# The q, k and v products of a windowed attention layer, from f32 matmuls to three f32r terms

## What is computed

```
h   = emb[x] + 2 * (lora_A[:, x].T @ lora_B.T)
n   = layernorm(h)
q, k, v = split(n @ Wqkv + bqkv)            # 16 heads of 16
local   = softmax over keys within 64 tokens of the query, times v
global  = softmax over the first 64 keys, times v of the first 64 tokens
h   = h + ((1 - g) * local + g * global) @ Wout + bout,  g = sigmoid(n @ Wg + bg)
h   = h + ffn(layernorm(h))                  # 8 experts, 2 per token, capacity 1.25
```

## Time and profile before

| | |
|---|---|
| Median of 3 runs | 3883.29 us (3879.36 to 3885.97) |
| The profiled execution: its own time | 3882.32 us |
| Its span, first to last instruction | 3880.6 us |
| PE busy | 3481.5 us (90% of the span), 47537 matmuls |
| PEld busy | 2753.0 us (71%), 47537 loads |
| DVE, ACT, POOL busy | 2172.5 (56%), 1868.3 (48%), 2324.1 us (60%) |
| Mean granted clock of PE | 0.952 |

### The profile page before, as it was taken

How to read it: one execution, slowest core, us unless ns; L and a number is a source line. 1 busy time by engine, 2 the same in 40 slices (tenths; PEclk the granted TensorE clock), 3 DMA queues, 4 the chain that set the end, 5 groups by cost and what they waited for, 6 DMA issues and landing times. The chain is left out here.

```text
span 3880.6 us, 117579 instructions
## 1 busy us (share of the span) xinstructions
PE 3481.5 (90%) x47537; PEld 2753.0 (71%) x47537; DVE 2172.5 (56%) x5392; ACT 1868.3 (48%) x3086; POOL 2324.1 (60%) x2599
## 2 busy tenths in 40 slices
PE   2898889888888888888899849999999999999998
PEld 1555555555555555555555539999999999999998
DVE  3576767767676776767677634343434344443333
ACT  0455555555555555555555624343444444444343
POOL 5566777777777777777776645444544444444443
PEclk7899999999999999999999969999999999999999
DMA  4354544445454444545454323232323233222222
GB/s 142 123 157 117 163 122 151 130 138 139 128 152 123 150 133 135 144 125 149 124 154 130 109 87 65 50 68 46 71 48 72 48 69 72 46 51 45 45 45 41
DMA packets 242540, 398.31 MB, mean 103 GB/s; under 512 B 34572, under 2 KB 150748, under 8 KB 242044
## 3 DMA queue, kind: packets, MB, share of 16 engines
q1 hardware_dynamic: 168540, 297.43, 25.0%
q0 software_dynamic: 70512, 91.16, 13.8%
q10 hardware_dynamic: 3008, 2.95, 0.2%
HBM read 198.55 MB, written 192.88 MB: 101 GB/s over the span
## 5 line engine op out<-in xcount | busy, mean ns | idle before, releaser
L1388 POOL DMA_INDIRECT out_y<-out_t,tok_out x264 | 425.7, 1612 | 747.3 <-DMA out_y<-out_t,tok_out 405.0
L1534 ACT ACTIVATE act<-psS 128x512 f32<-128x512 f32 x528 | 316.9, 600 | 882.1 <-PE psS L1462 880.9
L1596 DVE TENSOR_TENSOR h_lo<-act,h_hi 128x512 fp32r<-128x512 f32 x528 | 367.2, 695 | 562.3 <-ACT h_hi L1535 543.8
L993 DVE TENSOR_REDUCE negm<-psS 128x4 f32<-128x640 f32 x512 | 418.8, 818 | 452.3 <-remote 276.3
L903 ACT ACTIVATE pl<-psS 128x896 f32<-128x896 f32 x512 | 467.7, 913 | 379.9 <-PE psS L741 372.0
L568 POOL TENSOR_SCALAR_AFFINE_SELECT pl<-pl 128x512 f32<-128x512 f32 x512 | 354.3, 692 | 448.4 <-ACT pl L903 446.2
L1497 PE MATMUL psO<-w_hi,h_hi 128*128 128x256 f32 x2112 | 598.8, 284 | 0.8 <-DVE h_lo L1596 0.8
L1497 PE MATMUL psO<-w_lo,h_hi 128*128 128x256 f32 x2112 | 588.7, 279 | 0.0
L1497 PE MATMUL psO<-w_hi,h_lo 128*128 128x256 f32 x2112 | 587.6, 278 | 0.0
L1462 PE MATMUL psS<-xg_hi,w_hi 128*128 128x256 f32 x1984 | 551.7, 278 | 0.0
L1462 PE MATMUL psS<-xg_hi,w_lo 128*128 128x256 f32 x1984 | 551.5, 278 | 0.0
(11 more groups left out here) (232 smaller groups left out, 7728.6 us busy)
## 6 DMA issues: line engine op xcount, KB each, us to landing
qk_scr<-qk SPq DMA_DIRECT2D x64, 768.0 KB
Q<-qk_scr SPq DMA_DIRECT2D x128, 384.0 KB
K<-qk_scr SPq DMA_DIRECT2D x128, 384.0 KB
qk_scr<-qk SPq DMA_DIRECT2D x64, 512.0 KB
qk_scr<-qk SPq DMA_DIRECT2D x64, 256.0 KB
h_rows<-held SPq DMA_DIRECT2D x32, 512.0 KB
hb<-h_rows SPq DMA_DIRECT2D x32, 512.0 KB
x_rows<-x SPq DMA_DIRECT2D x32, 512.0 KB
```

Source lines behind the costliest of these rows:

```text
L993: dve.tensor_reduce(negm[:, g, 0, v, :, 2 * half:2 * half + 2], psS[:, 2:4, 0:2 * BAND].rearrange("p a (q u) -> p a q u", u=BAND), AX.X, A ...
L1388: pool.indirect_dma_start(out=y[:, :], in_=out_t[:, tile.out, s, :], in_offset=None, out_offset=bass.IndirectOffsetOnAxis(ap=tok_out[:, ti ...
L1534: act.activation(act32[:, b, :, 0:cols], src, ACT.Silu)
L1596: dve.tensor_tensor(h_lo[:, 2 * b:2 * b + 2, 0:cols], act32[:, b, :, 0:cols], h_hi[:, 2 * b:2 * b + 2, 0:cols].bitcast(F32), ALU.subtract) ...
```

## The change

- The weights of q and k (`wqk`) and of v (`wv_sb`) become two F32R tiles each, `*_hi` (the rounded value) and `*_lo` (what is left), made in the setup by DVE.
- The transposed rows `xn_t` become `xn_hi` and `xn_lo`, both F32R. ACT writes `xn_hi` from the PSUM bank and DVE, in a new stage `xn_lo`, subtracts it from the bank into `xn_lo`. PE's later stages wait for `xn_lo_done`, and the bank is free only then.
- Each product becomes three matmuls: hi by hi, and the two of hi by lo.
- Both row tiles have 64 more columns in front that repeat the first 64 tokens. So `values` 2 takes 128 columns of rows (the first 64 tokens twice) as weights against all 256 columns of `wv`, in 6 matmuls where there were 4 products (8 instructions), and ACT picks its half of the columns.
- All five lists in `ORDER` are laid out anew, and their starting points move, which is why some flags differ. POOL's is shown whole; of PE's and DVE's the stretch around `xn_t` and `qk`.

```diff
-        wv_sb = keep("wv_sb", [P, KT, D])
+        wv_hi = keep("wv_hi", [P, KT, D], F32R)
+        wv_lo = keep("wv_lo", [P, KT, D], F32R)
...
-        wqk = keep("wqk", [P, KT, 4, P])
+        wqk_hi = keep("wqk_hi", [P, KT, 4, P], F32R)
+        wqk_lo = keep("wqk_lo", [P, KT, 4, P], F32R)
...
+                    dve.tensor_copy(wv_hi[:, :, :], wv_raw[:, :, :])
                     for k in range(KT):
                         for s in range(2):
-                            dve.tensor_copy(wqk[:, k, 2 * s:2 * s + 2, :].rearrange("p a (d h) -> p a d h", d=HD),
-                                            wqk_raw[:, k, s * D:(s + 1) * D].rearrange("p (h a d) -> p a d h", a=2, d=HD))
+                            ins = dve.tensor_copy(wqk_hi[:, k, 2 * s:2 * s + 2, :].rearrange("p a (d h) -> p a d h", d=HD),
+                                                  wqk_raw[:, k, s * D:(s + 1) * D].rearrange("p (h a d) -> p a d h", a=2, d=HD))
+                    ins.then_inc(w_cut, 1)
+                    dve.wait_ge(w_cut, 1)
+                    dve.tensor_tensor(wv_lo[:, :, :], wv_raw[:, :, :], wv_hi[:, :, :].bitcast(F32), ALU.subtract)
+                    for k in range(KT):
+                        for s in range(2):
+                            dve.tensor_tensor(wqk_lo[:, k, 2 * s:2 * s + 2, :].rearrange("p a (d h) -> p a d h", d=HD),
+                                              wqk_raw[:, k, s * D:(s + 1) * D].rearrange("p (h a d) -> p a d h", a=2, d=HD),
+                                              wqk_hi[:, k, 2 * s:2 * s + 2, :].rearrange("p a (d h) -> p a d h", d=HD).bitcast(F32),
+                                              ALU.subtract)
...
-            xn_t = tmp("xn_t", [P, KT, T])
+            xn_hi = tmp("xn_hi", [P, KT, SIDE + T], F32R)
+            xn_lo = tmp("xn_lo", [P, KT, SIDE + T], F32R)
...
-                            wv = wv_sb[:, :, :].rearrange("p k (v a d) -> p k a v d", a=2, d=HD)
-                            pe.wait_ge(xn_t_done, KT * (s + 1))
+                            pe.wait_ge(xn_lo_done, KT * (s + 1))
                             take(key, v_done, 3 * s + arg + 1)
                             if arg < 2:
                                 for j in range(2):
-                                    tok = slice((2 * arg + j) * P, (2 * arg + j + 1) * P)
+                                    tok = slice(SIDE + (2 * arg + j) * P, SIDE + (2 * arg + j + 1) * P)
                                     for k in range(KT):
-                                        last = pe.matmul(psX[:, b, j * D:(j + 1) * D], xn_t[:, k, tok], wv_sb[:, k, :],
-                                                         start=(k == 0), stop=(k == KT - 1))
+                                        for n, (x_, w) in enumerate(((xn_hi, wv_hi), (xn_hi, wv_lo), (xn_lo, wv_hi))):
+                                            last = pe.matmul(psX[:, b, j * D:(j + 1) * D], x_[:, k, tok], w[:, k, :],
+                                                             start=(k == 0 and n == 0), stop=(k == KT - 1 and n == 2))
                             else:
                                 for k in range(KT):
-                                    for a in range(2):
-                                        last = pe.matmul(psX[64 * a:64 * (a + 1), b, 0:P], xn_t[:, k, 0:64], wv[:, k, a, :, :],
-                                                         start=(k == 0), stop=(k == KT - 1))
+                                    for n, (x_, w) in enumerate(((xn_hi, wv_hi), (xn_hi, wv_lo), (xn_lo, wv_hi))):
+                                        last = pe.matmul(psX[:, b, 0:D], x_[:, k, 0:2 * SIDE], w[:, k, :],
+                                                         start=(k == 0 and n == 0), stop=(k == KT - 1 and n == 2))
                             last.then_inc(v_ready, 1)
...
-                            take(key, xn_t_done, KT * s + arg + 1)
+                            take(key, xn_lo_done, KT * s + arg + 1)
...
-                            pe.wait_ge(xn_t_done, KT * (s + 1))
+                            pe.wait_ge(xn_lo_done, KT * (s + 1))
                             take(key, qk_rest_done, 4 * s + arg + 1)
                             for k in range(KT):
-                                last = pe.matmul(psX[:, b, :], wqk[:, k, arg, :], xn_t[:, k, :],
-                                                 start=(k == 0), stop=(k == KT - 1))
+                                for n, (w, x_) in enumerate(((wqk_hi, xn_hi), (wqk_hi, xn_lo), (wqk_lo, xn_hi))):
+                                    last = pe.matmul(psX[:, b, :], w[:, k, arg, :], x_[:, k, SIDE:SIDE + T],
+                                                     start=(k == 0 and n == 0), stop=(k == KT - 1 and n == 2))
                             last.then_inc(qk_ready, 1)
...
-                                                         psX[rows, b, 0:P].rearrange("p (v d) -> p v d", d=HD), ACT.Copy)
+                                                         psX[rows, b, 0:D].rearrange("p (v a d) -> p v a d", a=2, d=HD)[:, :, a, :], ACT.Copy)
...
-                            act.activation(xn_t[:, arg, :], psX[:, b, :], ACT.Copy).then_inc(xn_t_done, 1)
+                            act.activation(xn_hi[:, arg, 0:SIDE], psX[:, b, 0:SIDE], ACT.Copy)
+                            act.activation(xn_hi[:, arg, SIDE:SIDE + T], psX[:, b, :], ACT.Copy).then_inc(xn_hi_done, 1)
...
+                        if stage == "xn_lo":
+                            dve.wait_ge(xn_hi_done, KT * s + arg + 1)
+                            if arg == 0:
+                                need(dve, v_ready, 3 * s)
+                                need(dve, qk_ready, 4 * s)
+                            x_ = psX[:, BANK["xn_t", arg, s], :]
+                            dve.tensor_tensor(xn_lo[:, arg, 0:SIDE], x_[:, 0:SIDE], xn_hi[:, arg, 0:SIDE].bitcast(F32), ALU.subtract)
+                            dve.tensor_tensor(xn_lo[:, arg, SIDE:SIDE + T], x_, xn_hi[:, arg, SIDE:SIDE + T].bitcast(F32),
+                                              ALU.subtract).then_inc(xn_lo_done, 1)
...
 ORDER["pe"]
-                ("nxt", "max", 11), ("far", "xn_t", 0), ("far", "xn_t", 1), ("nxt", "exp", 0), ("nxt", "max", 12), ("far", "qk", 0),
-                ("nxt", "exp", 1), ("far", "qk", 1), ("far", "qk", 2), ("nxt", "max", 13), ("far", "qk", 3), ("nxt", "exp", 2),
...
+                ("nxt", "m_rows", 1), ("cur", "out", 11), ("nxt", "values", 2), ("far", "xn_t", 0), ("nxt", "max", 11),
+                ("far", "xn_t", 1), ("nxt", "exp", 0), ("nxt", "max", 12), ("nxt", "exp", 1), ("far", "qk", 0), ("far", "qk", 1),
+                ("nxt", "max", 13), ("far", "qk", 2), ("far", "qk", 3), ("nxt", "exp", 2), ("nxt", "max", 14), ("cur", "mix", 0),
...
 ORDER["dve"]
-                ("nxt", "kg", 2), ("prev", "top", 0), ("nxt", "max", 11), ("nxt", "max", 12), ("far", "qk", 0), ("far", "zgate", 0),
-                ("far", "qk", 1), ("prev", "top", 1), ("far", "qk", 2), ("nxt", "max", 13), ("far", "qk", 3), ("nxt", "max", 14),
...
+                ("nxt", "max", 11), ("far", "xn_lo", 0), ("far", "xn_lo", 1), ("past", "rank", 5), ("prev", "top", 2),
+                ("nxt", "max", 12), ("nxt", "kg", 0), ("far", "qk", 0), ("far", "qk", 1), ("nxt", "max", 13), ("prev", "top", 3),
+                ("far", "qk", 2), ("far", "qk", 3), ("nxt", "max", 14), ("cur", "mix", (0, 0)), ("nxt", "cut", (2, 0)),
...
             ORDER["pool"] = (
-                ("nxt", "hold", 0), ("far", "gather", 5), ("cur", "sel", 0), ("cur", "sel", 1), ("nxt", "hold", 1),
-                ("nxt", "qk3", 0), ("nxt", "qk3", 1), ("nxt", "qk3", 2), ("nxt", "qk3", 3), ("cur", "sel", 2), ("prev", "mix", 0),
-                ("cur", "sel", 3), ("old", "scatter", 4), ("old", "scatter", 5), ("prev", "mix", 1), ("cur", "sel", 5),
-                ("cur", "sel", 6), ("prev", "mix", 2), ("prev", "mix", 3), ("far", "gather", 6), ("cur", "sel", 7),
-                ("nxt", "hold", 2), ("cur", "sel", 8), ("far", "gather", 7), ("old", "scatter", 6), ("nxt", "hold", 3),
-                ("cur", "sel", 10), ("old", "scatter", 7), ("cur", "sel", 11), ("cur", "sel", 12), ("prev", "rstd2", None),
-                ("cur", "sel", 13), ("past", "scatter", 0), ("past", "scatter", 1), ("cur", "sel", 15), ("cur", "sel", 16),
-                ("cur", "sel", 17), ("next", "gather", 0), ("far", "rstd1", None), ("cur", "sel", 18), ("next", "gather", 1),
-                ("past", "scatter", 2), ("next", "gather", 2), ("next", "gather", 3), ("past", "scatter", 3), ("next", "gather", 4),
+                ("prev", "sel", 12), ("prev", "sel", 13), ("past", "rstd2", None), ("far", "gather", 0), ("prev", "sel", 15),
+                ("prev", "sel", 16), ("prev", "sel", 17), ("nxt", "rstd1", None), ("prev", "sel", 18), ("far", "gather", 1),
+                ("far", "gather", 2), ("far", "gather", 3), ("far", "gather", 4), ("old", "scatter", 0), ("nxt", "hold", 0),
```

(6 more changed lines are left out.)

98 lines of the change are left out of this document (50 added, 48 removed).

## The result

The changed kernel takes 3894.9 us, median of 12 runs (3880.3 to 3914.5). The kernel before takes 3879.1 in its 12 (3873.8 to 3888.3). The ratio is **1.0042**, 95% interval 1.0024 to 1.0059: a little slower, where the forecast was 3835 and faster. The profiled execution has a span of 3897.1 us, 16.5 more than before. Its marker line runs from 274.4 to 2289.1 (before, 268.2 to 2272.3): 6.2 us come ahead of the first marker and 10.6 between the first and the last, 0.34 a sequence. The expert part, with the same code, has the rest, -0.3.

What follows compares the result with a forecast made beforehand. PE was taken to bound the attention part (886.0 of 1000 us busy). Terms of -1.6 us a sequence, 32 times, gave -51 us; with +3 for setup and +1, 3882.3 became 3835 us, range 3775 to 3905.

Steps and rivals of the forecast that it cites:

- The products as such: PE's q and k products: 24 f32r matmuls at 0.27 us a step, 6.5 us a sequence in place of 8.4.
- The lists: 0: New order of all lists priced at 0 us a sequence (-1.0 to +1.5); POOL's run of seven stays, three pairs become four scatters.
- the clock falls a second time in a period: Sign that the forecast is wrong: the four scatters in a row bring a second low clock in each period.
- my first rival: Late hop: ACT's and DVE's signals each 1.9 us late, +1.6 us a sequence, 3937 us; chance 0.18 with milder forms and scatters.
- PE time taken out is on the path: At the qk stages other engines wait for PE, so PE time saved there shortens the period.
- My terms for the arithmetic: For one sequence: q and k -1.9, values -0.7 and +0.3, hop +0.6, DVE's extra work +0.1; sum -1.6 us.
- The values' -0.4: PE's value products: values 0 and 1 -0.7 us a sequence, values 2 +0.3.
- q and k's -1.9: q and k products gain 1.9 us a sequence (1.5 to 2.3), with 20% of steps slow before and after.
- The hop: +0.6: New ACT-to-DVE-to-PE step xn_lo ahead of qk costs 0.6 us a sequence (+0.2 to +1.3).
- The rival of "hidden": POOL's burst and the maxima around it end the period, PE waits longer for negm; no change, 3886 us, chance 0.10.
- Setup: Five subtractions and a copy on DVE in the setup add 3 us once.
- the third rival: Weight loads not hidden: each product term adds its 188 ns load, +8.8 us a sequence, 4168 us; chance 0.02.

Runs made afterwards that it cites:

- f32_new_lists: Kernel before (old arithmetic) with the changed kernel's lists, without the xn_lo steps; 3671.4 us on a quiet chip, 3949.3 us on a stalling one.
- changed_again_2: The changed kernel as it is, run again on a quiet chip; 3643.5 us against 3677.8 for the kernel before.
- terms_old_lists_2: The changed arithmetic with the old lists, xn_lo put behind max 11, on a stalling chip; 3889.7 us against 3893.0 for the kernel before, 0.9993.

## Why the prediction was wrong

*The products as such: the step was nearly right, the size hangs on the clock.* 0.242 us a step on average (median 0.232), where I had 0.27, and 0.228 at the high clock. The mean is even above my upper bound of 0.238, since the first step of a stage takes 0.34 (1332.86 to 1333.20). Line 812's steps have the priced 0.12. In the result q and k gained 3.0 us, not 1.9, because none of them lies under the low clock any more. Where no step is at half speed in either arithmetic, as in `f32_new_lists` and `changed_again_2` on quiet chips, the gain is 16 x 0.444 - 24 x 0.242 = 1.3, and 1.1 in the table (7.24 to 6.16). I had kept 20% of slow steps for both.

*"The lists: 0", with the run of seven that "stays": the step that failed.* I set three followers in pairs against three in a row of four and called it even, left the run of seven at nothing, and added the terms one by one. What a run costs depends on which stages wait beside it. In the kernel before, `max` 11 and the transpositions stood there. In the changed one it is ACT's copy of `values`, PE's `values` 2 behind it (25.7 us of waiting in 1000, 1.7 before), and the logits; and the four scatters stand on `attn_t` and `project`. The stalls cost the changed kernel 7.6 us a sequence where they cost the kernel before 6.7 on the same two chips: +0.9 where I had 0. Without stalls the lists' 0 is right (0.9999). With the old arithmetic and stalls the term is +56 us / 32 = +1.75 us a sequence, outside my -1.0 to +1.5; with the changed arithmetic it is 0 again, and there it is the arithmetic's -1.6 that measures -0.1. So it is the adding of separate terms beside a stall that was wrong, whichever order they are taken in.

*The sign "the clock falls a second time in a period" was met by half.* The fall in the middle of the period is there, beside the four scatters, and 8 products of `project` take 3.76 us behind it against 1.99. But the fall behind the run of seven is gone in most periods, so it is still about one a period, and 99 us of low clock in place of 167. Only with the old arithmetic in the new lists does the clock fall twice. That the four scatters would bring the low clock in another place stood in my first rival, as a side remark, and that remark came true.

*"PE time taken out is on the path": right on quiet chips.* With the same lists there (`f32_new_lists` and `changed_again_2`, two chips) the stretches change by -0.40 up to `xn_t`, +0.19 up to the first product, -1.08 over the products, +0.02 and +0.21 behind, -1.05 us in all. My terms for the arithmetic add up to -1.6. The values' -0.4 came true, the hop was priced too high, and q and k's -1.9 was too much where there is no low clock.

*The hop: +0.6 was too much for the new lists (it is nearly nothing) and too little for the old.* There PE waits 1.2 us a sequence for `xn_lo` on a quiet chip and 0.65 behind a stall, where the whole stretch is 1.6 longer. Two delays of 1.9 us, the mechanism of my first rival, are in no trace; the new lists have `xn_t` behind the run. The rival of "hidden", 3886, is nearest the measured time, but not for its reason: there PE was to wait longer for `negm`, and PE's wait for it only goes from 32.6 to 39.6 us in 1000.

*Setup.* Priced +3 us; the first q product starts at 78.4 instead of 74.3, 4.1 later.

*Weight loads.* They stay hidden: loads of 188 ns under steps of 0.242 and 0.12 us, the same row group throughout. The Trainium skill ("TensorE: Matmul & The Clock Gate", Part 3, The mechanism) has a rule that a weight load overlaps a running matmul only where the row group differs, by which the third rival would have come; the trace disagrees with it again. The same section also has loads into a background weight buffer pulled ahead; whether these are such loads, no run here shows.

So the balance is: -1.1 us a sequence of arithmetic, and +0.9 because the stalls cost the changed kernel 7.6 in place of 6.7. That gives the -6 us of the stalling chip; it is the same four times written another way and no test of the account. The chip of the result gave +16, and the 22 us between the two stay open.

## What to carry to other kernels

A row of indirect transfers on POOL is not a cost of POOL's: price it by the stages of the other engines that stand beside it, and price it anew when lists are laid out again, even if the row itself stays. Where a profile has long waits for remote beside such a row, set the transfers apart before anything else: one edit of one list gave 5.7% on a stalling chip, and the arithmetic about 1% on a quiet one. On quiet chips setting parts of the transfers apart cost the changed kernel 0.6 to 1.1%, so such an edit has to be timed on both kinds. Beside a stall, don't add up terms that were priced one by one: the same change of arithmetic was worth 3 us in one set of lists and about 60 in another. And measure on more than one chip: a gain can be there on one and gone on the next.

## What was not expected of the hardware

- The same program takes 3671 us on some chips and 3893 on others. For the changed kernel, which was traced on both kinds, the difference is all in the attention part: the last marker comes at 2284.0 and 2030.3 us, and the rest takes 1605.7 and 1607.7. What the traces show beside it is waits for remote while POOL issues transfers in a row: DVE 8.0 us in `terms_old_lists_2` and before, ACT 8.4 in the changed kernel, and none on the other chips. Setting the transfers apart takes the kernel before to 3668 us on a stalling chip.
- One transfer with an operation of POOL's on either side leaves hardly a wait on a stalling chip, seven in a row stall for 8 us, and each of them takes POOL 1.0 us in either case.
- The shorter products in the same lists came with a longer low clock behind the stall: 235 us instead of 167 in 1600 us, at the lower of its two levels. PE has less work there and also a later start, and which of the two does it was not separated. Ahead of the fall at 1360.9 us PE had waited, with 1.1 of 3 us busy.
- ACT waits 8.4 us beside a row of transfers (at `values`, where it reads a bank of PSUM and writes its own tile). "SBUF — State Buffer" in the Trainium skill, section SBUF: two separate sides, says that among the engines only DVE's and GpSimd's shared port pair is contended, and that PE and ACT never wait on anyone. The trace does not say what ACT waits for here, so it neither bears the rule out nor refutes it. The cause was not found.
